# A fused decoder layer on one core: the feed-forward's turns and Hadamard products in the banks of the gates, its down weights shared by three engines, and a new order around the key projection

## The reference, cut to what matters

```
x = x + cross_attention(layernorm(x), ctx of 4096 tokens)   # 16 heads of 32; q, k, v, p fake-quantized
x = x + latent_attention(layernorm(x))                      # 16 heads of 128, rotary part of 64
x = x + ffn(layernorm(x))

act_quant(x)    = clip(round(x * s), -128, 127) / s,  s = 128 / max|x| per token
weight_quant(w) = clip(round(w * s), -1, 1) / s,      s = 1 / mean|w| over the whole matrix
gate, up = act_quant(x) @ weight_quant(w_gate).T, act_quant(x) @ weight_quant(w_up).T     # 512 -> 2048
h        = fwht(silu(gate) * up)        # Walsh-Hadamard over 2048, times 2048 ** -0.5
out      = act_quant(h) @ weight_quant(w_down).T                                          # 2048 -> 512
```

## Time and profile before

| | |
|---|---|
| three timed runs | 637.55, 640.27, 642.52 us (median 640.27) |
| the profiled execution's own time | 637.43 us |
| its span, first to last instruction | 635.6 us |
| busy over the span: PE, DVE, ACT, POOL | 86%, 76%, 59%, 6% |
| mean granted clock of TensorE | 0.936 of 2.4 GHz |
| second attention's last output projection ends | 562.29 us |

### The profile page before, as it was taken

One profiled execution on the slowest core, in us unless ns is written; L12 is line 12 of the kernel. 1 busy time (PEld: TensorE's weight loads), 2 busy tenths in 40 slices (PEclk: granted clock), 3 DMA queues, 4 the chain that ended last, 5 costly groups with the idle time before them and its releaser, 6 DMA issues. The chain is left out here.

```text
span 635.6 us, 10683 instructions
## 1 busy us (share of the span) xinstructions
PE 546.7 (86%) x4318; PEld 346.4 (55%) x4318; DVE 483.3 (76%) x880; ACT 372.1 (59%) x392; POOL 36.9 (6%) x30
## 2 busy tenths in 40 slices
PE   2899999997999899889977886799997999934787
PEld 1344555544556555555555664488884656611374
DVE  2599999957999899989997993202663895977795
ACT  5525564448889799979878784101126474562343
POOL 0200000002000200110020000000000000036000
PEclk9999999999999999999997665899999999985979
DMA  9523200053434434424542797000606605100000
GB/s 326 208 68 121 78 1 1 1 182 134 134 133 135 133 134 138 162 102 160 163 164 78 275 402 296 0 1 1 264 1 264 265 0 200 67 0 1 0 1 33
DMA packets 18896, 76.67 MB, mean 121 GB/s; under 512 B 1952, under 2 KB 3104, under 8 KB 16800
## 3 DMA queue, kind: packets, MB, share of 16 engines
q1 hardware_dynamic: 18848, 76.00, 33.1%
HBM read 75.20 MB, written 0.79 MB: 120 GB/s over the span
## 5 line engine op out<-in xcount | busy, mean ns | idle before, releaser
L1036 DVE CUSTOM_DVE_ANT_0 arena<-ps,arena 128x1024 f32<-128x1024 f32 x128 | 153.9, 1219 | 16.0 <-issue 9.4
L1398 ACT ACTIVATE arena<-arena,small 128x4096 int16<-128x4096 f32 x32 | 121.8, 3805 | 0.0
L599 PE MATMUL ps<-small,arena 128*128 128x128 bf16 x1024 | 88.3, 236 | 22.8 <-ACT arena L1398 14.8
L558 PE MATMUL ps<-arena 128*128 128x512 f16 x384 | 99.9, 380 | 0.0
L524 PE MATMUL ps<-arena 128*128 128x512 f16 x384 | 85.2, 379 | 1.0 <-DVE arena L967 0.9
L599 PEld LDWEIGHTS ps<-small,arena 128*128 128x128 bf16 x1024 | 65.6, 105 | 35.8 <-ACT arena L1398 17.2
L1405 ACT ACTIVATE arena<-ps 128x1024 bf16<-128x1024 int16 x64 | 65.5, 1024 | 31.1 <-PE ps L599 30.8
L731 PE MATMUL ps<-arena 128*128 128x256 f32 (+1 forms) x288 | 68.7, 398 | 0.7 <-ACT arena L1468 0.7
L731 PEld LDWEIGHTS ps<-arena 128*128 128x128 f32 x288 | 55.8, 194 | 11.8 <-issue 3.3
L524 PEld LDWEIGHTS ps<-arena 128*128 128x128 f16 x384 | 37.1, 98 | 43.3 <-issue 1.3
L615 PEld LDWEIGHTS ps<-arena 128*128 128x128 bf16 x1024 | 43.5, 99 | 29.4 <-issue 5.0
(11 more groups left out here) (153 smaller groups left out, 750.6 us busy)
## 6 DMA issues: line engine op xcount, KB each, us to landing
arena<-key_scales SPq DMA_DIRECT2D x64, 512.0 KB, 4.7
arena<-in_ctxT SPq DMA_DIRECT2D x8, 1024.0 KB, 5.5
arena<-in_wg SPq DMA_DIRECT2D x1, 4096.0 KB, 12.0
arena<-in_wo SPq DMA_DIRECT2D x1, 4096.0 KB, 12.0
arena<-in_wu SPq DMA_DIRECT2D x1, 4096.0 KB, 22.0
arena<-in_wd SPq DMA_DIRECT2D x4, 1024.0 KB, 6.0
arena<-in_wuq SPq DMA_DIRECT2D x1, 3072.0 KB, 24.4
arena<-in_wkr SPq DMA_DIRECT2D x1, 2048.0 KB, 12.4
```

The lines of the kernel that those rows point to most:

```text
L558: last = pe.matmul(ps[:, bank, :], wv16[wpart][:, k, g * P:(g + 1) * P], ctx16[cpart][:, k, tok], start=(k == 0 and i == 0), stop=(k == KC ...
L599: last = pe.transpose(ps[:, bank, :].bitcast(BF16)[:, b * P:(b + 1) * P], p16[u % 2][:, (8 * q + b) * P:(8 * q + b + 1) * P].bitcast(BF16) ...
L1036: dve.tensor_tensor_reduce(sc[:, u % 2, i * SCW:(i + 1) * SCW], ps[:, 2 * (n % 2):2 * (n % 2) + 2, :].rearrange("p a b -> p (a b)"), skb[: ...
L1398: act.activation(p16[u % 2], sc[:, u % 2, :], ACT.Exp, bias=ebias[:, u % 2:u % 2 + 1], scale=sq[:, i:i + 1], accum_out=rsum[:, u:u + 1]).t ...
```

## The change: what it does

Feed-forward:
- `variance` with the residual comes ahead of the wait for `wdm` and the down mean. ScalarE's list becomes `std(2)`, `scale_down(0)`, `(1)`, Silu's table, stores of xiT, `scale_down(2)`, Silu of n = 0, `scale_down(3)`, the other Silus.
- Down weights: blocks 0 and 1 are clipped and subtracted by DVE ahead of `gated(0)`, blocks 2 and 3 by GpSimd behind that (it waits for `wdv`).
- The second tile's xi is turned into bank 7, so the gates may start with the first tile's xiT alone.
- Butterflies have three stages; the fourth is done by the Hadamard product, for which the constant is 128x384 ([had, had, -had]) and each block streams 256 columns, two blocks adding into one half of a bank. The constant's load moves behind the up weights.
- Turns go to banks 0 and 1, Hadamard products to 2 and 3 (the gates' banks), down products to 4 and 5, so they wait for Silus and not for `gated`.
- The second tile's last row maximum is taken in three pieces, and ScalarE does half of its `to_units`.

Key projection and first steps:
- ScalarE: `bound(2)` ahead of `store_projected_queries`. DVE: `round_queries` behind the first half's evacuation.
- PE turns the scales ahead of the last quarter of the second value projection; ScalarE loads Exp's table early and stores the scales ahead of the first values.
- In step 0 only one value projection stands ahead of the scores 2, one behind it; ScalarE stores the last two value projections behind the first exponentials; in step 1 the values' scale, turns and stores come later.

```diff
-            for stage in range(4):
+            for stage in range(3):
                 src, dst = tt[stage % 2], tt[(stage + 1) % 2]
-                a, b = (m[:, t, :].rearrange("p (n two m w) -> p n two m w", two=2, m=1 << stage, w=P)
+                a, b = (m[:, t, :].rearrange("p (n two m w) -> p n two m w", two=2, m=2 << stage, w=P)
...
             out.append(("p", s - 2, 3))
-            out += [("v", g, 3)] if half == 1 else [("v", g, 0)] if half == 0 else []
+            out += [("v", g, 3)] if half == 1 else [("v", g, 0)] if half == 0 and g else []
             out.append(("p", s - 1, 0))
             if half == 0:
+                out.append(("v", g, 1 if g else 0))
+            out.append(("p", s - 1, 1))
+            if half == 0 and not g:
                 out.append(("v", g, 1))
...
-            sp.dma_start(had_sb, had).then_inc(ld_const, 16)
...
             sp.dma_start(wu32, wu).then_inc(ld_u, 16)
+            sp.dma_start(had_sb, had).then_inc(ld_const, 16)
...
-                project_values(g, j, i, range(KC))
+                project_values(g, j, i, range(KC - 1))
                 if i == 1:
                     turn_scales()
+                project_values(g, j, i, range(KC - 1, KC))
...
-                for g, j, bank in steps[:2] if s == 0 else []:
+                for g, j, bank in steps[:1] if s == 0 else []:
                     project_values(g, j, bank, range(KC))
...
                 if now:
                     scores(s, 2)
+                for g, j, bank in steps[1:2] if s == 0 else []:
+                    project_values(g, j, bank, range(KC))
...
             for t in range(QT):
                 pe.wait_ge(xis, t + 1)
                 for k in range(KC):
-                    last = pe.transpose(ps[:, 4 + t, :].bitcast(BF16)[:, k * P:(k + 1) * P],
+                    last = pe.transpose(ps[:, 4 + 3 * t, :].bitcast(BF16)[:, k * P:(k + 1) * P],
...
             pe.wait_ge(tern, 24)
-            pe.wait_ge(xie, QT)
             for n in range(QT * 4):
                 t, c = n // 4, n % 4
+                if n == 0:
+                    pe.wait_ge(xie, 1)
+                elif n == 3:
+                    pe.wait_ge(xie, QT)
...
                 else:
-                    pe.wait_ge(gd, 7 + n)
+                    pe.wait_ge(ga, 7 + n)
                 for b in range(4):
-                    last = pe.matmul(ps[:, 6 + n % 2, b * P:(b + 1) * P], uT[:, n % 2, b, :], had_sb,
-                                     start=True, stop=True)
+                    last = pe.matmul(ps[:, 2 + n % 2, b // 2 * N:(b // 2 + 1) * N], uT[:, n % 2, b, :],
+                                     had_sb[:, b % 2 * P:(b % 2 + 2) * P], start=(b % 2 == 0), stop=(b % 2 == 1))
...
-                    pe.wait_ge(bfd, 8 * t + (7 if n % 4 < 2 else 8))
+                    pe.wait_ge(bfd, 6 * t + (5 if n % 4 < 2 else 6))
                     if n >= 2:
                         pe.wait_ge(ue, n - 1)
                     else:
-                        pe.wait_ge(gd, 5 + n)
+                        pe.wait_ge(ga, 5 + n)
...
                 low_part(i)
-                if j == 1:
-                    round_queries()
                 key_evacuate(j - 1, 0)
...
                 key_units(j - 1, 0)
+                if j == 1:
+                    round_queries()
...
+            variance(x1, residual2)
             dve.wait_ge(wdm, 1)
             link(dve.tensor_reduce(wmean[:, 2:3], ps[:, 4, N:N + 4], AX, ALU.add))
             mean_of(2, wmean[:, 2:3])
             dve.sem_inc(wdsc, 1)
-            layernorm(x1, xn3, 2, residual2)
+            normalize(x1, xn3, 2)
...
+            for k in range(2):
+                dve.wait_ge(wdch, k + 1)
+                dve.tensor_scalar(wd32[k], wd32[k], MAGIC + 1.0, MAGIC - 1.0, ALU.min, ALU.max).then_inc(wdclip, 1)
+            for k in range(2):
+                dve.wait_ge(wdclip, k + 1)
+                dve.wait_ge(tern, 24)
+                dve.tensor_scalar(wdb[k], wd32[k], -MAGIC, None, ALU.add).then_inc(wdv, 1)
...
-            for k in range(4):
+
+            pool.wait_ge(wdv, 2)
+            for k in (2, 3):
                 pool.wait_ge(wdch, k + 1)
                 pool.tensor_scalar(wd32[k], wd32[k], MAGIC + 1.0, MAGIC - 1.0, ALU.min, ALU.max).then_inc(wdclip, 1)
-            for k in range(4):
                 pool.wait_ge(wdclip, k + 1)
-                pool.wait_ge(tern, 3 * (KC + (3 if k < 2 else 4)))
+                pool.wait_ge(tern, 24)
                 pool.tensor_scalar(wdb[k], wd32[k], 1.0, -MAGIC, ALU.mult, ALU.add).then_inc(wdr, 1)
...
             high_part(1)
+            bound(2)
             store_projected_queries()
-            bound(2)
...
+            act.activation(exp_table[:, :], id32[:, 0:1], ACT.Exp)
+            store_scales()
             for i, (g, j) in enumerate(FIRST_V):
                 store_projected_values(g, j, i)
-                if i == 1:
-                    store_scales()
...
                 if prev:
                     exponentials(s - 1)
+                if s == 1:
+                    for g, j, bank in value_steps(0)[2:]:
+                        store_projected_values(g, j, bank)
...
             act.wait_ge(ones_s, 2)
-            scale_down(0)
-            scale_down(1)
             std(2)
-            scale_down(2)
-            scale_down(3)
+            for k in range(2):
+                scale_down(k)
             act.activation(junk[:, 0:1], ones[:, 0:1], ACT.Silu).then_inc(achain, 1)
...
+            scale_down(2)
             act.wait_ge(wum, 1)
...
+                if n == 0:
+                    scale_down(3)
...
             for t in range(QT):
+                if t:
+                    act.wait_ge(asc, t + 1)
+                    act.activation(y_sb[:, t, I // 2:], y_sb[:, t, I // 2:], ACT.Identity, scale=ascale[:, t:t + 1],
+                                   bias=magic[:, 0:1]).then_inc(yun, 1)
```

More of the change, by code:

```diff
@@ L151, in build @@
         rinv = small([UNITS])
+        exp_table = small([1])
         ps = es.enter_context(nc.psum_tensor("ps", [P, 8, 512], F32))
@@ L250, in build @@
         amax = small([QT])
-        ahalf = small([QT, 2])
+        apart = small([QT, 3])
         ascale = small([QT])
@@ L686, in _ @@
                     values(s - 2, 2)
-                if half == 0:
+                if half == 0 and group:
                     turn_values(group, 0)
@@ L1112, in _ @@
                     scale_scores(s, 0)
-                if half == 0:
-                    for g, j, _ in last[-2:]:
+                if half == 0 and s > 1:
+                    for g, j, _ in last:
                         max_values(g, j)
@@ L1118, in _ @@
                     scale_scores(s, 1)
+                if s == 1:
+                    for g, j, _ in last[2:]:
+                        max_values(g, j)
+                    scale_values(group)
                 if late:
@@ L1444, in _ @@
                 if s == 0:
-                    for g, j, bank in steps:
+                    for g, j, bank in steps[:2]:
                         store_projected_values(g, j, bank)
@@ L1459, in _ @@
                     store_pT(s - 1, 1)
+                if s == 1:
+                    store_values(group, 1)
             for t in range(QT):
@@ L1572, in constants @@
     eye = np.eye(P, dtype=f)
-    return dict(ident=eye, rotate=rotate, cosT=np.ascontiguousarray(cos), sinT=np.ascontiguousarray(sin), had=had)
+    return dict(ident=eye, rotate=rotate, cosT=np.ascontiguousarray(cos), sinT=np.ascontiguousarray(sin),
+                had=np.concatenate([had, had, -had], 1))
 def kernel(x, ctx_2048, L0_xattn_Wq, L0_xattn_bq, L0_xattn_Wkv, L0_xattn_bkv, L0_xattn_Wp, L0_xattn_bp,
```

45 lines of the change are left out of this document (27 added, 18 removed).

## The result

The changed kernel takes 623.1 us (median, 621.37 to 624.25), the kernel before 639.39 in the same sittings (637.55 to 642.52): a ratio of 0.974 with an interval of 0.969 to 0.979. The profiled execution took 621.37 us, against 637.43 before, so 16.06 us are to be found.

The account below looks back on a forecast made before the run. It took the feed-forward chain after the last output projection as the main bound, with VectorE held by GpSimd. Feed-forward 14.1, keys 2.1 and first steps 0.6 sum to 16.8 us: 620.6 or 623.5, taken as 623, range 617 to 629.

Parts of the forecast that it names:

- GpSimd's hold on VectorE: Before the gates: two pairs of VectorE instructions took 4.05 and 4.04 us waiting on GpSimd; 0.42 us each with GpSimd idle.
- The square root's table load goes off the path: Before the feed-forward's norm: ScalarE is idle, so the 1.28 us load runs ahead of its wait and leaves the chain.
- Leg (a): Stretch from the last output projection to the first gate: gates start at 571.8 instead of 582.50, 10.7 us earlier.
- Butterflies: Feed-forward, after the gated products: one stage less per tile, saving 2.39 us twice; second tile's fifth instruction done at 598.9.
- Doubled product: Feed-forward Hadamard products: 256 columns a block make a tile's turns and products 8.85 us instead of 7.5, giving back 1.3.
- Nothing for the scale split and for the cover of the moved blocks: Feed-forward: ScalarE's half of to_units gains nothing; VectorE's moved down-weight blocks finish 1.1 us before the first silu, costing nothing.
- Keys: Key projection: TensorE starts keys 2.9 us sooner, of which 2.1 us reach the first values; bounds 0 and 2.9.
- First steps: First attention steps: third exponentials move from 163.34 to 160.6, worth 0.6 us beyond the keys; bounds -1 and +2.
- 1: Rival: GpSimd's hold on VectorE moves to the butterflies, 3.9 us come back, giving 627; chance 0.10.
- 2: Rival: early gains at keys and first steps are swallowed, only the feed-forward counts, giving 626; chance 0.12.
- 3: Rival: TensorE stays at 1.2 GHz from the feed-forward's first turn on, costing up to 24.9 us, giving 648; chance 0.03.
- 4: Rival: ScalarE reloads tables between Identity and Silu, first tile's silus end 2 us later, giving 625.5; chance 0.05.

Follow-up runs that it names:

- pool_all: Changed kernel with all four blocks of down weights clipped and subtracted on GpSimd again, none on VectorE; 627.55 us, ratio 0.981.
- before_pool_late: Kernel before, with one added wait so GpSimd starts on the down weights only after VectorE finishes xi and its scales; 633.06 us, ratio 0.990.
- tables_both: Changed kernel with the wait on constants moved behind the square root and Silu's dummy call behind the stores of xiT; 622.26 us, ratio 0.973.
- old_banks: Changed kernel with turns in banks 4 and 5 and Hadamard products in 6 and 7 again; 627.58 us, ratio 0.980.
- no_split: Changed kernel without ScalarE's share of the second tile's rounding and without the row maximum in three pieces; one execution, 624.03 us.
- before_keys: Kernel before with only the edits ahead of the key projection (second context bound earlier, queries rounded later); 636.65 us, ratio 0.994.
- four_stages: Changed kernel with four butterfly stages and 128-column Hadamard products again, in the new banks; 625.29 us, ratio 0.977.
- ffn_best: Changed kernel with earlier square-root table load, 30 unused TensorE products ahead of xi, and down block 3 later on ScalarE and GpSimd; 619.16 us, ratio 0.967.
- all_best: Changed kernel with ffn_best's edits plus one unused TensorE product per empty slot in the first attention's last eight units; 618.82 us, ratio 0.967.

## Why the prediction was right

It said 623 and 16.8 us off; 623.1 and 16.06 came. That the sum is so close is in part luck. The gates came 0.85 us later than reckoned, the part from gates to down products gained 0.5 less and the first steps 0.9 less; against that the keys gave 0.8 more, and 0.7 came from a stretch that had no term and differs that much between executions. The mechanisms below are what can be called right.

- **GpSimd's hold on VectorE**: right, and the largest cause. pool_all lost 5.6 us with it back, before_pool_late won 7.0 by taking it alone away.
- **The square root's table load goes off the path**: wrong, and the one step that failed. It rested on a layer norm whose activation has one wait. Here two waits stand ahead of the activation, one on constants, long met, and one on the variance, and the load ran behind the latter, at 561.60. It sat in the chain for 1.28 us; tables_both, with a single wait, has it at 555.81. Leg (a) gave 9.85 instead of 10.7.
- **Butterflies**: right, 1.22 us each, and the fifth releases the turns of both tiles. The gaps ahead of them are 0.90 and 0.42 us, where 0.7 and 1.0 were foretold; that the first tile's turns begin behind the fifth butterfly needed the new banks, which old_banks prices at 3.8 us. The prediction had this gain inside the butterflies' and gave it no term.
- **Doubled product**: 9.41 us a tile instead of 8.85. From the start of the turns to the first product it is 1.34 us, in which the first turn and its store stand one behind the other, where two turns of 0.44 and about 0.2 of wait were reckoned; and the first product takes 1.99 us, not 1.72. It gave back 1.9 us, not 1.3. Gates to down gained 2.91, not 3.4.
- **Nothing for the scale split and for the cover of the moved blocks**: right. no_split has the same stretch, and VectorE waited 0.94 us for the first silu behind its four blocks (1.1 foretold).
- **Keys**: mis-sized, 2.92 us instead of 2.1. round_queries takes 3.8 us, not 4.5, and its place costs nothing: in either order VectorE runs it and the evacuation of block 0's first half as one row of work without a gap, and that row begins at 29.19 instead of 32.10.
- **First steps**: 0.6 foretold, -0.31 against the old order at full clock, 1.15 and 2.34 against two executions of it that lost the clock. The foretold start of the third exponentials, 160.6, came at 160.73; how it is made up was wrong.
- **Rivals**: 1 is a true mechanism, 2.7 us in before_pool_late, 1.7 in tables_both and 0.2 here, so it did not decide. 2 is refuted by before_keys. 3, a clock that stays low through the feed-forward, did not come; but its cheaper form, a half clock behind a gap of 2 to 4 us, cost old_banks and four_stages part of their loss. Its premise, that in the trace of before the clock falls only behind gaps of over 2 us, was misread: from 330 to 380 us it stands at 0.5 to 0.8 (over 10 us each) with gaps of 0.4 to 1.5 us, and in the runs it also fell behind 1.82 and 1.29 us. 4 is false: no load stands between the silus.

## What to carry to other kernels

When VectorE instructions end at the same moments as GpSimd's, their durations are waits: compare each with the same shape where GpSimd is idle, and move GpSimd's work to where VectorE reads PSUM or has nothing due. In tables_both the next stage came 2.4 us sooner and met it there, so look at both ends. When a wait of two microseconds ahead of TensorE goes, count the clock behind it as well, though it is not lost in every execution; and when a table load is meant to run early, look at all the waits that stand before its activation.

## What the runs showed of the hardware

- **A hold lasts to the end of the other engine's instruction, whatever the held one's size.** VectorE's 128x2 tensor_scalar took 1.40 us instead of 0.17 and ended 0.02 us behind GpSimd's. GpSimd's were held too: 2.95 us instead of 1.90 in tables_both, and in the changed kernel 2.97 instead of 1.05 at 27.14 us, off the path. Not every VectorE instruction is held. In the kernel before these two ran side by side, and the statistics kept the 0.69 us that they take in the changed kernel, where GpSimd is idle:

```profile
565.33 3.88 POOL L1322 TENSOR_SCALAR arena<-arena 128x2048 f32<-128x2048 f32 x2 [231.99 <-ACT arena L1511]
...
565.38 0.69 DVE L902 BATCH_NORM_STATS2 small<-arena 128x6 f32<-128x512 f32 x1
```

  A reciprocal at 568.77 (0.17 us), in the second of the two, and the gated products (0.75 us, one input in PSUM) were not held either.
- **A table load can wait for what its activation waits for.** With two waits before the activation the load ran behind the later one, after 6.96 us of idle time; with one it ran at once. The Trainium skill (ScalarE: Activation LUTs, What ACT_TABLE_LOAD costs) puts a switch of tables at 2.66 us, load and drain. Here the activation behind the load at 567.08 started at 568.38, so 1.3 us, and the measurement decides.
- **The same instructions, behind the same gap, keep the full clock in one execution and lose it in another**: the same 64 products took 13.97 us in ffn_best and 15.66 in all_best, which differ only far ahead of them. Without unused products they took 16.39 us in the changed kernel, behind a wait of 8.46 us for xi, and 15.32 in pool_all, behind one of 14.43: the longer wait did not cost more. In the last steps of the first attention, profiled executions of the same code differ by up to 2.7 us (58.42 to 61.12 us).
